# A four-layer graph network on one core: source scores looked up with a stationary table, edge scores computed in a dense product

## The reference, cut to what matters

```
xp    = (x @ W).reshape(n, H, OUT)
a_src = einsum('nhc,hc->nh', xp, att_src)      # one score per node and head
a_dst = einsum('nhc,hc->nh', xp, att_dst)
a_edge = einsum('ehc,hc->eh', (ea2 @ W_edge).reshape(-1, H, OUT), att_edge)
alpha = leaky_relu(a_src[row2] + a_dst[col2] + a_edge)
attn  = exp(alpha - segment_max(alpha, col2)[col2]);  attn /= segment_sum(attn, col2)[col2]
agg   = segment_sum(attn[:, :, None] * xp[row2], col2)
```

## Time and profile before

| what | us |
|---|---|
| median of 3 runs | 3294.28 |
| the profiled execution's own time | 3291.56 |
| its span | 3290.0 |
| PE, DVE, ACT, POOL busy | 2399.1, 1562.5, 701.8, 1437.9 |
| first to last gather (L896) | 1988.2 to 3116.3 |
| DMA moved | 627.41 MB |

### The profile page before, as it was taken

One profiled execution on the slowest core, in us unless ns is written; L12 is line 12 of the kernel. 1 busy time (PEld: TensorE's weight loads), 2 busy tenths in 40 slices (PEclk: granted clock), 3 DMA queues, 4 the chain that ended last, 5 costly groups with the idle time before them and its releaser, 6 DMA issues. The chain is left out here.

```text
span 3290.0 us, 68610 instructions
## 1 busy us (share of the span) xinstructions
PE 2399.1 (73%) x21724; PEld 2069.6 (63%) x21725; DVE 1562.5 (47%) x3763; ACT 701.8 (21%) x1091; POOL 1437.9 (44%) x1498
## 2 busy tenths in 40 slices
PE   2799999899999944999969992655630104999965
PEld 2666666688688823888858881655630104999954
DVE  5576666523211173111133336888879102545567
ACT  0187778745100141000010000000000100000033
POOL 4522222223000021122224447777778777766665
PEclk9899999989899966999989995887765555555577
DMA  5588988832888716888689985988962534655611
GB/s 157 138 260 274 281 270 282 286 91 67 252 283 281 225 49 217 253 248 249 208 245 289 292 252 148 191 191 183 190 155 72 166 106 122 149 144 143 143 34 43
DMA packets 560774, 627.41 MB, mean 191 GB/s; under 512 B 265887, under 2 KB 412524, under 8 KB 560041
## 3 DMA queue, kind: packets, MB, share of 16 engines
q1 hardware_dynamic: 258425, 387.60, 38.7%
q10 hardware_dynamic: 252072, 164.25, 19.7%
q0 software_dynamic: 50208, 74.70, 9.4%
HBM read 484.61 MB, written 142.11 MB: 190 GB/s over the span
## 5 line engine op out<-in xcount | busy, mean ns | idle before, releaser
L896 POOL DMA_INDIRECT rows<-x_rows,src_i x832 | 853.4, 1026 | 281.8 <-issue 235.8
L1586 PE MATMUL ps<-slices,wide 128*128 128x250 f16 x7350 | 827.9, 271 | 42.8 <-DMA slices<-adjacency 42.7
L1586 PEld LDWEIGHTS ps<-slices,wide 128*128 128x128 f16 x7350 | 716.3, 98 | 130.3 <-issue 24.2
L1818 PE MATMUL ps<-slices 128*128 128x75 bf16 x4992 | 239.0, 223 | 170.2 <-DVE slices L2614 170.2
L1818 PEld LDWEIGHTS ps<-slices 128*128 128x128 bf16 x4992 | 232.5, 115 | 176.7 <-issue 176.7
L931 POOL TENSOR_TENSOR ea_one<-ea,ones 128x64 f32<-128x64 f32 x250 | 140.0, 561 | 428.0 <-DMA ea<-in_edge_attr 411.2
L1526 PE MATMUL ps<-weighted,slices 128*128 128x57 f32 x1120 | 253.3, 417 | 69.7 <-DVE weighted L2194 69.5
L1526 PEld LDWEIGHTS ps<-weighted,slices 128*128 128x128 f32 x1120 | 247.2, 333 | 70.2 <-DVE weighted L2194 69.8
L1467 PE MATMUL ps<-rows,weighted 128*32 128x128 f32 x2000 | 282.7, 288 | 8.7 <-DMA ea<-in_edge_attr 6.8
L1526 PE MATMUL ps<-weighted,rows 128*128 128x57 f32 x544 | 130.6, 419 | 195.3 <-DMA rows<-x_rows,src_i 170.3
L1526 PEld LDWEIGHTS ps<-weighted,rows 128*128 128x128 f32 x544 | 123.4, 332 | 198.2 <-issue 170.5
(11 more groups left out here) (356 smaller groups left out, 3423.7 us busy)
## 6 DMA issues: line engine op xcount, KB each, us to landing
slices<-adjacency SPq DMA_DIRECT2D x525, 437.5 KB, 5.3
rows<-in_edge_attr SPq DMA_DIRECT2D x250, 256.0 KB
adjacency<-wide ACTq DMA_DIRECT2D x91, 437.5 KB, 3.2
adjacency<-slices ACTq DMA_DIRECT2D x84, 437.5 KB, 3.1
x_of_edges<-rows SPq DMA_DIRECT2D x140, 256.0 KB
slices<-x_of_edges ACTq DMA_DIRECT2D x140, 256.0 KB
slices<-src_low ACTq DMA_DIRECT2D x52, 512.0 KB
rows<-x_rows,src_i POOLq DMA_INDIRECT x832
```

What stands on the lines that cost most here:

```text
L896: pool.indirect_dma_start(out=packed[i][:, c, :], out_offset=None, in_=table, in_offset=bass.IndirectOffsetOnAxis(ap=rows_of, axis=0)).the ...
L1586: mm = pe.matmul(ps_d[b], high_low[:, part, QS * s + q, :], slices[:, s, PN * q:PN * (q + 1)], start=(s == 0 and q == 0 and part == 0), st ...
L1818: mm = pe.matmul(ps_g[:, s, b, c, 0:HEADS * QH], lowT[:, s, b, h, P * c:P * (c + 1)], tab_b[:, n, h, :, :].rearrange("p h i -> p (h i)"), ...
```

## The change

It has four parts.

**Score lookup.** The low part is now the source modulo 384 as fp16, the high part a byte. The table (102 columns: a high and a low fp16 part, 3 heads, 17 high parts) is what PE holds, and the one-hot of the low parts streams through it in pieces of 512 columns (12 products a pass). The low list is loaded as one row, spread over the partitions by PE (4 products, `spread_low`) and copied by ACT. DVE makes 3 compares and 2 selections of 102 x 1024 (`score_step`), and PE adds the selected rows (4 products, `sum_picks`). ACT copies and stores the result with 3 transfers a pass. Table values are scaled by a power of two found in `score_scale`.

**Edge scores.** They leave the lookup. In the dense product `d2a` SP issues, ahead of slice 5 of each block, a load of 32 edges of each of 127 partitions (2048 bytes a row), and DVE multiplies and sums them (`edge_scores`). A 26th load follows the last block. The last partition has fewer edges; they come in one load of 128 x 80 numbers, their scores are stored and put in place later.

**Groups.** FRESH is 100 and STORED 108. The first 8 groups summed are stored ones, then 25 cycles of 8 with stored and fresh in turn. The waits for `scores_begun` are gone.

**The source list's parts** (early in the kernel) take 7 DVE operations and two stores instead of 3 and one.

```diff
+            def load_ea(c, i):
+
+                to = rows[0:P - 1, 1 + i, :, :].rearrange("p c f -> p (c f)")[:, 0:ESC * EF].rearrange("p (j e) -> p j e", e=EF)
+                sp.dma_start(to, ea16[0:(P - 1) * EPP, :].rearrange("(p j) e -> p j e", j=EPP)[:, bass.ds(ESC * c, ESC), :]
+                             ).then_inc(es_in[i], 16)
...
                     for s in range(SL):
+                        if k == 1 and s == SL - 2:
+                            if not first:
+                                sp.wait_ge(es_made, 2 * q - 1)
+                            load_ea(q, b)
...
+                if k == 1:
+                    sp.dma_start(ea_end, ea16[E - P * EST:E, :].rearrange("(p j) e -> p j e", j=EST)).then_inc(es_in[0], 16)
                 pairs(sp, body)
+                if k == 1:
+                    sp.wait_ge(es_made, 2 * NP - 1)
+                    load_ea(NP, NP % 2)
...
-                    pool.wait_ge(group_summed, SUMMED + place(0, 3 * (g - RING - STORED) + 2) + 1)
-                if SCORES_LEAD <= g < SCORES_LEAD + PASSES:
-                    pool.wait_ge(scores_begun, g - SCORES_LEAD + 1)
+                    pool.wait_ge(group_summed, SUMMED + place(0, 2 * (g - RING - STORED) + 1) + 1)
...
+            def copy_low(u, s, b, first=False):
+
+                act.wait_ge(low_spread, 2 * u + b + 1)
+                if not first:
+                    act.wait_ge(lowT_ready, u - 1)
+                act.activation(low[:, s, SH * b:SH * (b + 1)], ps_s, ACT.Copy).then_inc(low_copied, 1)
+
+            def store_as(k, s, first=False):
+
+                u = 2 * k + s
+                act.wait_ge(picks_summed, 2 * u + 2)
+                if not first:
+                    act.wait_ge(as_stored[s], 16 * HEADS * k)
+                act.activation(as_o[:, s, :], ps_o[s], ACT.Copy).then_inc(as_copied, 1)
+                act.wait_ge(as_copied, u + 1)
+                for h in range(HEADS):
+                    act.dma_start(as_d[h:h + 1, bass.ds(SB * u, SB)].rearrange("h (j e) -> (h j) e", e=SQ), as_o[4 * h:4 * (h + 1), s, :]
+                                  ).then_inc(as_stored[s], 16)
...
-            def score_rows(k, s, b):
-
-                pe.wait_ge(lowT_ready, 2 * k + s + 1)
-                pe.wait_ge(picked_ready, 4 * k + 2 * s + b + 1)
-                for c in range(BC):
-                    for h in range(KT):
-                        for n in range(3):
-                            mm = pe.matmul(ps_g[:, s, b, c, 0:HEADS * QH],
-                                           lowT[:, s, b, h, P * c:P * (c + 1)],
-                                           tab_b[:, n, h, :, :].rearrange("p h i -> p (h i)"),
-                                           start=(h == 0 and n == 0), stop=(h == KT - 1 and n == 2))
-                            if c == 0 and h == 0 and n == 0:
-                                mm.then_inc(scores_begun, 1)
+            def score_rows(u, s, b, first):
+
+                pe.wait_ge(lowT_ready, u + 1)
+                if not (first and s == 0):
+                    pe.wait_ge(picked_ready, 2 * u + b - 1)
+                for h in range(KT):
+                    for c in range(2):
+                        mm = pe.matmul(ps_g[:, b, SQ * c:SQ * (c + 1)], tab_b[:, h, :, :, :].rearrange("p n h i -> p (n h i)"),
+                                       lowT[:, s, h, SH * b + SQ * c:SH * b + SQ * (c + 1)], start=(h == 0), stop=(h == KT - 1))
                 mm.then_inc(g_summed, 1)
 
+            def sum_picks(u, s, b, first):
+
+                pe.wait_ge(picked_ready, 2 * u + b + 1)
+                if b == 0 and not first:
+                    pe.wait_ge(as_copied, u - 1)
+                for c in range(2):
+                    j = 2 * b + c
+                    mm = pe.matmul(ps_o[s], gather_up[0:QR, j, :], picked[:, b, SQ * c:SQ * (c + 1)], start=(j == 0), stop=(j == 3))
+                mm.then_inc(picks_summed, 1)
+
+            def spread_low(k, s, b, first=False):
+
+                u = 2 * k + s
+                if b == 0:
+                    pe.wait_ge(low_in[s], 16 * (k + 1))
+                if not (first and s == 0 and b == 0):
+                    pe.wait_ge(low_copied, 2 * u + b)
+                for c in range(2):
+                    mm = pe.matmul(ps_s[:, SQ * c:SQ * (c + 1)], ones_h[:, :], low_rows[:, s, SH * b + SQ * c:SH * b + SQ * (c + 1)],
+                                   start=True, stop=True)
+                mm.then_inc(low_spread, 1)
...
+                v.tensor_scalar(low_i, lists[1], 7, None, ALU.arith_shift_right).then_inc(dve_step, step.up())
+                v.wait_ge(dve_step, step.n)
+                v.tensor_copy(hi_f, low_i).then_inc(dve_step, step.up())
+                v.wait_ge(dve_step, step.n)
+                v.tensor_scalar(low_i, hi_f, 21846.0, None, ALU.mult).then_inc(dve_step, step.up())
+                v.wait_ge(dve_step, step.n)
+                v.tensor_scalar(low_i, low_i, 16, None, ALU.arith_shift_right).then_inc(dve_step, step.up())
+                v.wait_ge(dve_step, step.n)
+                v.tensor_copy(hi_list, low_i).then_inc(low_ready3, 1)
+                v.tensor_copy(hi_f, low_i).then_inc(dve_step, step.up())
+                v.wait_ge(dve_step, step.n)
+                v.scalar_tensor_tensor(low_list, hi_f, -float(HI_DIV), lists_f[1], ALU.mult, ALU.add).then_inc(low_ready3, 1)
+                v.wait_ge(low_ready3, 2)
...
+            def products(n, frm, count, p):
+
+                of = es_prod[0:p, :, 0:count, :]
+                v.tensor_tensor(of, frm.unsqueeze(1).to_broadcast([p, HEADS, count, EF]),
+                                we_b[0:p, :, :].unsqueeze(2).to_broadcast([p, HEADS, count, EF]), ALU.mult).then_inc(es_made, 1)
+                v.wait_ge(es_made, 2 * n + 1)
+                return of
+
+            def edge_scores(c, u, i):
+
+                ea_c = rows[0:P - 1, 1 + i, :, :].rearrange("p c f -> p (c f)")[:, 0:ESC * EF].rearrange("p (j e) -> p j e", e=EF)
+                v.wait_ge(es_in[i], 16 * (u + 1) + (16 if i == 0 else 0))
+                if isinstance(c, int) and c == 0:
+                    v.tensor_reduce(es_end[:, :, :], products(0, ea_end, EST, P), AX.X, ALU.add).then_inc(es_made, 1)
+                v.wait_ge(es_made, 2 * c + 2)
+                v.tensor_reduce(es[0:P - 1, :, bass.ds(ESC * c, ESC)], products(c + 1, ea_c, ESC, P - 1), AX.X, ALU.add).then_inc(es_made, 1)
 
             def layer2(q, u, s, first):
 
@@ -2539,6 +2688,7 @@
                 if not first:
                     v.wait_ge(d2a.H, H1 * (q - 1))
                 mean(d2a, q, s)
+                edge_scores(q, u, s)
...
+            def lows(u, s):
+
+                v.wait_ge(low_copied, 2 * u + 2)
                 for k in range(KT):
-                    op = v.tensor_scalar(lowT[:, s, :, k, :], low[:, s, :].rearrange("p (b e) -> p b e", b=2),
-                                         slot_p[:, k:k + 1], None, ALU.is_equal)
+                    op = v.tensor_scalar(lowT[:, s, k, :], low[:, s, :], slot_p[:, k:k + 1], None, ALU.is_equal)
                 op.then_inc(lowT_ready, 1)
 
-            def score_step(k, s, last):
+            def score_step(k, s, first=False, last=False):
 
                 u = 2 * k + s
                 if not (last and s == 1):
-                    lows(16 * (k + 1 + s), 1 - s)
-                for b in range(2):
-                    v.tensor_tensor(sel[:, b, :, :], key[:, bass.ds(NC * u + BC * b, BC)].unsqueeze(2).to_broadcast([P, BC, QH]),
-                                    iota_h[:, :].unsqueeze(1).to_broadcast([P, BC, QH]), ALU.is_equal).then_inc(sel_ready, 1)
-                for i in range(RING):
-                    v.wait_ge(ea_landed[i], 16 * (u + 1))
-                v.tensor_tensor(prod[:, :, :, :, :].rearrange("p i c h e -> p (i c) h e"),
-                                ea[:, :, :, :].rearrange("p i c e -> p (i c) e").unsqueeze(2).to_broadcast([P, NC, HEADS, EF]),
-                                we_b[:, :, :].unsqueeze(1).to_broadcast([P, NC, HEADS, EF]), ALU.mult).then_inc(prod_ready, 1)
+                    lows(u + 1, 1 - s)
+                v.wait_ge(hi_in[s], 16 * (k + 1))
                 for b in range(2):
                     v.wait_ge(g_summed, 2 * u + b + 1)
-                    v.wait_ge(sel_ready, 2 * u + b + 1)
-                    v.tensor_tensor(picked[:, b, :, :, :],
-                                    ps_g[:, s, b, :, 0:HEADS * QH].rearrange("p c (h i) -> p c h i", h=HEADS),
-                                    sel[:, b, :, :].unsqueeze(2).to_broadcast([P, BC, HEADS, QH]), ALU.mult).then_inc(picked_ready, 1)
-                v.wait_ge(prod_ready, u + 1)
-                v.tensor_reduce(e_score[:, :, :, :].rearrange("p i c h -> p (i c) h"),
-                                prod[:, :, :, :, :].rearrange("p i c h e -> p (i c) h e"), AX.X, ALU.add).then_inc(e_ready, 1)
-                for b in range(2):
```

(99 more changed lines are left out.)

284 lines of the change are left out of this document (153 added, 131 removed).

## The result

The changed kernel takes 3423.69 us (median of 4 runs, 3421.94 to 3428.70), the kernel before 3292.43 (3282.87 to 3296.93): the ratio is 1.0412, with a 95% interval of 1.0391 to 1.0432. It is 131 us slower. The profiled execution's span is 3423.0 us against 3290.0.

A forecast was written before the change was run, and what follows sets the result against it. PE was taken to bound `d2a`, within a row of successive stages. Terms +199 - 22.4 - 9 - 3 + 3.8 + 2.5 = +171 on 3291.56 gave 3462.5, with 2.7 for the median 3465 us; range 3390 to 3580.

The forecast's parts named there:

- the step that hung on the Trainium skill: Edge load in `d2a`: 127 partitions put everything on one engine, the same lowest-numbered one every time; block 21.9 us, +199 us.
- Rival A: In `d2a` the edge load spreads over the engines or goes to changing ones, PE stays the bound: 3266 us, chance 0.10.
- B: In `d2a` a MB on the one engine costs the heavy window's 52.8 us: +309, 3575 us in all, chance 0.12.
- C: In `d2a` PE, idle between slices, drops to half clock, 27.9 us a block: +349, 3615 us in all, chance 0.03.
- D: The score lookup runs at half clock, 10.0 us a pass: +88, 3553 us in all, chance 0.03.
- the price of a MB on that engine: In `d2a`, estimated at 44 us, low end 40; with 0.498 MB a block it gives 21.9 us a block and +199.
- The groups: In the attention stage's mixed sums, cycles of 8 remove POOL's waits for sums: -22.4 us, bounds 0 and -27.
- Behind the last gather: At the end of the attention stage no backlog of stored groups is left: -9 us, bounds -11 and 0.
- The lookup: Score lookup in the attention stage: pass of 5 to 7 us, length uncounted, less disturbance of gathers: -3 us, bounds -18 and +5.
- The small terms: Extra operations for the source list's parts, +3.8 us, and in the softmax and at the end of `d2a`, +2.5.
- the list's parts: Early in the kernel, 7 operations instead of 3, about 5.2 us against 1.45, ahead of POOL's next work: +3.8 us.
- The +2.5 for the softmax and the end of the product: One more softmax operation over all edges and a wait ending `d2a` for the 26th chunk: +2.5 us, from 0 to +12.

The follow-up runs named there:

- the split version: The changed kernel with each block's edge load cut into two transfers, partitions 0 to 111 and 112 to 126: 3253.64 us, 0.9902 of the kernel before.
- 122 rows: The changed kernel with an edge load of 122 rows instead of 127, scores of five partitions left out: 3291.73 us, 1.0013 of the kernel before.
- half the bytes: The changed kernel with 127 rows but 1024 instead of 2048 bytes of each: 3299.62 us, 1.0027 of the kernel before.
- the three primes: The changed kernel with the edge load cut into transfers of 41, 43 and 43 rows: 3901.30 us on another chip, 1.1195 of the kernel before there.
- the lookup alone: The changed kernel with its edge load split and the old grouping (68 fresh, 140 stored), without waits for score passes: 3291.87 us, 0.9994 of the kernel before.

## Why the prediction came out right

The forecast was 3465 us, the measurement 3424, the side and the mechanism as forecast.

The load of 127 rows runs on one transfer engine, and this engine sets the block: shown by the split version, by 122 rows, and by half the bytes. That it is the same engine each time is shown by the three primes. This was the step that hung on the Trainium skill ("DMA: Bandwidth & Descriptors", section "Why a DMA increments its semaphore by 16 and not by 1"): the trace agrees that it is always the same one, 20.52 us against 20.39; that it is the lowest-numbered, no row here shows. Rival A is out with it; what it described is the split version, 3266 in the prediction and 3253.64 measured. B, C and D did not come. The clock over the product did fall, from 1.00 to 0.88 with PE 79% busy, but PE still waited 93 us for slices at it, so the clock was not what set the block. The lookup ran in 297 us.

The term that was mis-sized is the price of a MB on that engine. I took 44 us, and 20.39 / 0.498 is 40.9, near the low end of 40. The prediction had 7.97 us a block more and +199; it was 6.45 us, 161 over 25 blocks, and the last block's copy came 162.0 us later. The 26th load cost nothing that can be seen: from that copy to the first gather it is 340.6 us now and was 342.3. The values of the kernel before that I leaned on, 47.7 and 52.8, were averages of all 16 engines of pieces of 1 KB, or in a crowd; a price for one engine that works alone on pieces of 2 to 3.5 KB was not among the rows, and I stayed too near them. The rows of the 26th load give it: 2048 bytes in 0.08 us are 39 us a MB. So the side and the mechanism were not luck; of the 41 us between forecast and measurement 37 are this one price.

The groups: POOL's waits -22.4 forecast, and the mixed sums' excess fell by 22.9. Behind the last gather -9, and it was -10.8 (18.1 to 7.3). Alone they gave 38 us by the medians (34 by the ratio, 26 to 43 by its interval), against 31 of the sum, or 36 with the 4.3 us of score waits that this kernel also drops. The prediction took the mixed sums' excess from 269 gathers as 27 us; the earlier trace rows has 270 in that window, so 25.5.

The lookup: -3 forecast, it was +7.4. That its length is worth nothing was right (the lookup alone, 0.9994). That a shorter one would disturb less was wrong: it does its disturbing in less time, and 4.3 us of what it was set against had been score waits. Its pass takes about 5.6 us, in the 5 to 7 that were given, and DVE's operations measured 0.75 and 1.27 us against 0.75 and 1.28.

The small terms: the list's parts take 5.5 us in a row, near the 5.2 of the forecast, yet the first window transfer goes out at 78.64 where it did at 78.00, since DVE came to them 3.3 us earlier. +3.8 was therefore 0.6. The +2.5 for the softmax and the end of the product does not show either: the scans' excess is 34.5 against 34.3. What is left, 2 us in the gap behind the product and 2 in the last layer, is as small as what single profiles vary by: the kernel with the groups alone has the same program up to the first gather and issues it at 1982.0 and not 1988.2.

## What to carry to other kernels

Count the rows of a transfer before its bytes: as one load, 127 rows cost 161 us over the 25 blocks here, and 170 in the whole time, that 112 and 15 did not. A mean share of the transfer engines hides one that is full; look for a busy engine waiting on loads while the mean has fallen. And a change of several parts is best run part by part: here one part gave 38 us, one gave nothing, and one took 170.

The version to keep is one of two that beat both kernels: the kernel before with the new groups (3252.90), or the changed one with its load split (3253.64).

## What the hardware showed beside that

One transfer engine took a packet of 2048 bytes every 0.08 us (26 GB/s), and one load of 127 rows, or three of 41, 43 and 43, never used a second one. A row of three compares that began 0.15 us ahead of a gather held it back by 0.48 us; the same row begun 0.2 us behind a gather's start, beside a selection, made it 3.09 us long; one such compare, 0.53 us behind the start, made it 2.10. A strided compare of 2048 fp16 columns took 1.41 us against 0.75. Beside selections that read PSUM the gathers mostly kept their 0.94 us, as long as no compare began in them.
